# One tower on one core: the first stage's scores and projection become one 384-column product in f16 halves, and pooling reads projected rows

## What is computed

```python
A = jnp.tanh(jnp.einsum('bst,dt->bsd', text_embeddings, W_w) + W_b + b)
scores = jnp.einsum('bsd,od->bso', A, V_w)[..., 0] + V_b[0]
starts = jnp.arange(0, S - patch_len + 1, stride)      # patch_len 4, stride 2
idx = starts[:, None] + jnp.arange(patch_len)
sw = scores[:, idx]
w = jax.nn.softmax(sw, axis=-1)
xw = text_embeddings[:, idx]
attended = jnp.einsum('bpl,bplt->bpt', w, xw)
return jnp.einsum('bpt,dt->bpd', attended, P_w) + P_b
```

## Time and profile before

| | |
|---|---|
| median of 3 runs | 2064.79 us |
| the profiled execution | 2065.83 us, span 2063.9 us |
| setup | 0 to about 26 us of the span |
| first stage | 26.11 us (first load of x) to 459.98 us (last product ends) |
| TensorE busy over the span | 93% |
| VectorE, ScalarE, GpSimd busy | 72%, 68%, 56% |
| granted TensorE clock, mean | 0.973 of full speed |

### The profile page before, as it was taken

How to read it: one execution, slowest core, us unless ns; L and a number is a source line. 1 busy time by engine, 2 the same in 40 slices (tenths; PEclk the granted TensorE clock), 3 DMA queues, 4 the chain that set the end, 5 groups by cost and what they waited for, 6 DMA issues and landing times. The chain is left out here.

```text
span 2063.9 us, 60351 instructions
## 1 busy us (share of the span) xinstructions
PE 1911.3 (93%) x20800; PEld 1179.2 (57%) x20800; DVE 1478.8 (72%) x3636; ACT 1410.4 (68%) x2978; POOL 1162.1 (56%) x2198
## 2 busy tenths in 40 slices
PE   3999999993999999999999999999991899999998
PEld 3999999980444444444444444444441566666666
DVE  4555555553899999999999999999981455555554
ACT  1333333330889899899898998998982666666665
POOL 1111111127677777777777777777756565565561
PEclk9999999995999999999999999999996899999999
DMA  4444444421444444444444444444440332322322
GB/s 138 127 114 117 121 122 122 122 62 29 80 89 89 88 90 88 90 88 90 90 86 90 90 90 89 89 88 90 87 80 13 57 64 62 71 62 63 71 63 52
DMA packets 512122, 176.03 MB, mean 85 GB/s; under 512 B 452169, under 2 KB 511308, under 8 KB 512076
## 3 DMA queue, kind: packets, MB, share of 16 engines
q1 hardware_dynamic: 512075, 175.43, 38.7%
HBM read 53.79 MB, written 12.48 MB: 32 GB/s over the span
## 5 line engine op out<-in xcount | busy, mean ns | idle before, releaser
L692 DVE TENSOR_REDUCE tops<-p_maxa 128x6 f32<-128x762 f32 x512 | 483.0, 943 | 61.9 <-PE p_maxa L534 60.7
L605 PE MATMUL p_o<-probs,vn 127*32 127x256 f32 x6144 | 410.7, 385 | 0.2 <-DVE att L720 0.2
L530 PE MATMUL p_s<-qm,kt 32*128 32x256 f16 x3072 | 399.1, 275 | 1.3 <-ACT probs L649 0.4
L646 ACT ACTIVATE probs<-p_s 128x512 f32<-128x512 f32 x512 | 305.4, 596 | 108.4 <-PE p_s L530 95.6
L694 DVE TENSOR_REDUCE tops<-p_maxb 128x4 f32<-128x508 f32 x512 | 346.4, 676 | 0.0
L652 ACT ACTIVATE probs<-p_s 128x512 f32<-128x512 f32 x512 | 309.4, 604 | 0.0
L649 ACT ACTIVATE probs<-p_s 128x512 f32<-128x512 f32 x512 | 304.9, 596 | 0.3 <-PE p_s L530 0.2
L966 DVE TENSOR_TENSOR gel_lo<-gel,gel_hi 128x512 f16<-128x512 f32 x192 | 147.4, 768 | 215.7 <-ACT gel_hi L956 214.4
L534 PE MATMUL p_maxa<-kt,qt 24*128 24x256 f16 (+1 forms) x2048 | 284.1, 250 | 16.0 <-DMA kt<-qk 8.5
L360 POOL TENSOR_TENSOR diag<-ident,weight 128x256 f32<-128x256 f32 x128 | 78.9, 617 | 369.2 <-DVE band L339 328.3
L530 PEld LDWEIGHTS p_s<-qm,kt 32*128 32x128 f16 x3072 | 134.7, 91 | 182.9 <-issue 168.6
(11 more groups left out here) (186 smaller groups left out, 4522.3 us busy)
## 6 DMA issues: line engine op xcount, KB each, us to landing
xn<-in_xn SPq DMA_DIRECT2D x32, 768.0 KB, 6.3
xt_a<-in_xt SPq DMA_DIRECT2D x32, 512.0 KB, 4.4
out<-out_sb SPq DMA_DIRECT2D x32, 336.0 KB, 2.7
xt_b<-in_xt SPq DMA_DIRECT2D x32, 256.0 KB, 5.2
xt<-hx SPq DMA_TRANSPOSE x128, 2.3
kt<-qk SPq DMA_TRANSPOSE x128, 2.7
qt<-qk SPq DMA_TRANSPOSE x128, 2.4
qm<-qk SPq DMA_TRANSPOSE x128, 2.7
```

Of the source, the lines that this page charges most:

```text
L530: return nc.tensor.matmul(o, kt[full(j), r, kind, g, :], qm[full(j), r % 2, versions, g, :], start=True, stop=True, skip_group_check=True)
L605: last = nc.tensor.matmul(p_o[32 * j:32 * j + 32, blocks, :], vn[0:NP, r, src:src + 32], probs[0:NP, r % 2, QUAD * g + j, kind * 256:(kind ...
L646: nc.scalar.activation(probs[:, r % 2, h + 1, 0:512], p_s[1][:, :, :].rearrange("p x n -> p (x n)"), ACT.Exp, scale=SCALE).then_inc(act_e1 ...
L692: nc.vector.tensor_reduce(top[:, q, pair, 4:10], p_ma[:, 0:6, 0:NP], AX.X, ALU.max, negate=True).then_inc(dve_ma[u], 1)
```

## The change

W and P stand side by side as one matrix of 384 columns, so that one product gives a row's hidden values (columns 0 to 191) and its projected row (columns 192 to 383). The product runs in f16: x is split into a high and a low f16 half (x = hi + lo to about f32 accuracy), and so are the weights. Channels 0 to 127 take three products (hi x hi, hi x lo, lo x hi); channels 128 to 191 are loaded twice, on partitions 0 to 63 and 64 to 127, so that one stationary tile xb holds their low half above their high half and two products do; one more product of a tile of ones with bt adds the biases. So a half of a batch takes six products of 384 columns (L231 to L236 of the new kernel), and each of the two pa buffers is now two PSUM banks. ScalarE takes tanh of the first 192 columns of each half (L281) and copies the other 192 to zs (L283), a buffer of two groups. The pooling is then one product for each half, band times zs, straight into ph (L254); pt, att and the load of xn are gone.

The halves of x are made on the chip, one group ahead and two batches at a time, at k = 0 and at k = 2: ScalarE writes xa_hi (L270) and the masked high half of xt_b (L272, buffer tmp, named xb_hi in the program); GpSimd subtracts twice (L376, L379). The setup makes the f16 halves of the weights, and some counters are merged.

The core of the diff:

```diff
-                        pe.wait_ge(act_tanh, seen(n - 1))
+                        if k % 2 == 0:
+                            pe.wait_ge(pool_split, seen(i * 4 + 2 + 2 * (k // 2)))
+                        pe.wait_ge(act_z, seen(n - 1))
                         for odd in range(2):
-                            o = pa[two][:, odd * C:(odd + 1) * C]
-                            nc.tensor.matmul(o, xt_a[:, par, k, odd * 128:(odd + 1) * 128], t.wt_a[:, :], start=True, stop=False)
-                            last = nc.tensor.matmul(o, xt_b[:, par, k, odd * 128:(odd + 1) * 128], t.wt_b[:, :], start=False, stop=True)
+                            o, cols = pa[two][:, odd, 0:2 * C], slice(odd * 128, (odd + 1) * 128)
+                            nc.tensor.matmul(o, xa_hi[:, par, k, cols], ahi[:, :], start=True, stop=False)
+                            nc.tensor.matmul(o, xa_hi[:, par, k, cols], alo[:, :], start=False, stop=False)
+                            nc.tensor.matmul(o, xa_lo[:, par, k, cols], ahi[:, :], start=False, stop=False)
+                            nc.tensor.matmul(o, ones16[:, :], t.bt[:, :], start=False, stop=False)
+                            nc.tensor.matmul(o, xb[:, par, k, cols], bhi[:, :], start=False, stop=False)
+                            last = nc.tensor.matmul(o, xb[:, par, k, cols], blo[:, :], start=False, stop=True)
                         last.then_inc(pe_a, 1)
...
                         pe.wait_ge(dve_band, seen(u + 1))
-                        pe.wait_ge(act_att, seen(u - 1))
-                        for odd in range(2):
-                            nc.tensor.matmul(pt[two][:, 0:128], xn[:, par, k, odd * C:odd * C + CA], band[:, two, odd, :],
...
                         pe.wait_ge(act_h, seen(u - 1))
+                        for odd in range(2):
+                            last = nc.tensor.matmul(ph[two][:, 0:C], band[:, two, odd, :], zs[:, par, k, odd, :],
+                                                    start=(odd == 0), stop=(odd == 1))
+                        last.then_inc(pe_h, 1)
...
+            def split(i, par, half, part):
+
+                if within(i + 1, NG):
+                    two = slice(2 * part, 2 * part + 2)
+                    if part == 0:
+                        act.wait_ge(xt_in[1 - par], seen((half + par) * 48 + 48))
+                        act.wait_ge(pe_a, seen(i * G))
+                    nc.scalar.activation(xa_hi[:, 1 - par, two, :], xt_a[:, 1 - par, two, :], ACT.Copy)
+                    act.wait_ge(pool_split, seen(i * 4 + 4 + 2 * part))
+                    nc.scalar.activation(tmp[:, :, :], xt_b[:, 1 - par, two, :], ACT.Identity, scale=mask[:, 0:1], bias=none[:, 0:1])\
+                        .then_inc(act_split, 1)
...
+                        act.wait_ge(pe_h, seen(n - 2 * G + 1))
+                        nc.scalar.activation(zs[:, par, k, :, :], pa[two][:, :, C:2 * C], ACT.Copy).then_inc(act_z, 1)
+                    if k % 2 == 0:
+                        split(i, par, half, k // 2)
...
+                    if k % 2 == 0 and within(i + 1, NG):
+                        both = slice(k, k + 2)
+                        pool.wait_ge(act_split, seen(i * 2 + 3 + k // 2))
+                        nc.gpsimd.tensor_tensor(xa_lo[:, 1 - par, both, :], xt_a[:, 1 - par, both, :], xa_hi[:, 1 - par, both, :], ALU.subtract)\
+                            .then_inc(pool_split, 1)
+                        pool.wait_ge(pool_split, seen(i * 4 + 5 + k))
+                        nc.gpsimd.tensor_tensor(xb[:, 1 - par, both, :], xt_b[:, 1 - par, both, :], tmp[:, :, :], ALU.subtract)\
+                            .then_inc(pool_split, 1)
```

More of the change, by code:

```diff
@@ L109, in _ @@
         def _(dve):
+            nc.vector.memset(t.bt[:, :], 0.0)
             nc.vector.memset(t.bproj[:, :], 0.0).then_inc(cleared, 1)
@@ L118, in _ @@
             nc.vector.tensor_copy(t.b2[:, :], b2f[:, :])
+            for k in range(2):
+                nc.vector.tensor_copy(t.wt[k][:, :], wtf[k][:, :])
+                for row in (64 * k, 64 * k + 32):
+                    nc.vector.tensor_copy(t.bt[row:row + 1, :], btf[row:row + 1, :])
             nc.vector.tensor_copy(t.bproj[0:1, :], bprojf[0:1, :])
@@ L126, in _ @@
             nc.vector.tensor_tensor(t.w2_lo[:, :, :], w2f[:, :, :], t.w2_hi[:, :, :], ALU.subtract)
+            for k in range(2):
+                nc.vector.tensor_tensor(t.wt[2 + k][:, :], wtf[k][:, :], t.wt[k][:, :], ALU.subtract)
+                row = 64 * k + 32
+                nc.vector.tensor_tensor(t.bt[row:row + 1, :], btf[row:row + 1, :], t.bt[row:row + 1, :], ALU.subtract)
             nc.vector.tensor_tensor(t.b2[96:128, :], b2f[96:128, :], t.b2[96:128, :], ALU.subtract)
@@ L143, in tokenize @@
         xt_a = sb("xt_a", [CA, 2, G, S])
-        xt_b = sb("xt_b", [CB + 2, 2, G, S])
-        xn = sb("xn", [128, 2, G, 2 * C])
+        xt_b = sb("xt_b", [128, 2, G, S])
+        xa_hi, xa_lo, xb = (sb(n, [128, 2, G, S], F16) for n in ("xa_hi", "xa_lo", "xb"))
+        tmp = sb("xb_hi", [128, 2, S], F16)
+        mask, none = sb("mask", [128, 1]), sb("none", [128, 1])
+        ones16 = sb("ones_f16", [128, 128], F16)
+        zs = sb("zs", [128, 2, G, 2, C])
         tanhs = sb("tanhs", [128, 2, 2 * C])
@@ L156, in tokenize @@
         band = sb("band", [128, 2, 2, 128])
[L157 to L160, removed]
+        pa = [ps(f"pa{i}", [128, 2, 512]) for i in range(2)]
         ph = [ps(f"ph{i}", [128, 512]) for i in range(2)]
@@ L213, in _ @@
         def _(pe):
-            pe.wait_ge(ones, 3)
+            pe.wait_ge(ones, 4)
+            ahi, bhi, alo, blo = t.wt
             def body(i, par, half):
@@ L240, in body @@
                     if within(u, NB):
[L242 to L243 removed]
                         pe.wait_ge(dve_band, seen(u + 1))
[L245 removed]
+                        pe.wait_ge(act_h, seen(u - 1))
                         for odd in range(2):
[L247 to L260 removed]
+                            last = nc.tensor.matmul(ph[two][:, 0:C], band[:, two, odd, :], zs[:, par, k, odd, :],
+                                                    start=(odd == 0), stop=(odd == 1))
+                        last.then_inc(pe_h, 1)
             loop(pe, body)
@@ L274, in body @@
                         nc.scalar.activation(expo[:, :, :], shifted[:, :, :], ACT.Exp).then_inc(act_exp, 1)
-                    u = n - 2 * G
-                    if within(u, NB):
-                        act.wait_ge(pe_att, seen(u + 1))
-                        act.wait_ge(pe_h, seen(u - 1))
-                        nc.scalar.activation(att_a[:, two, :], pt[two][:, 0:128], ACT.Copy)
-                        nc.scalar.activation(att_b[0:CB, two, :], pt[two][0:CB, 128:256], ACT.Copy).then_inc(act_att, 1)
                     u = n - 2 * G - 1
@@ L288, in _ @@
         def _(dve):
-            nc.vector.memset(xt_b[CB:CB + 2, :, :, :], 1.0).then_inc(ones, 1)
-            nc.vector.memset(att_b[CB:CB + 1, :, :], 1.0).then_inc(ones, 1)
+            nc.vector.memset(ones16[:, :], 1.0).then_inc(ones, 1)
+            nc.vector.memset(none[:, :], 0.0)
+            nc.vector.memset(mask[0:CB, :], 0.0).then_inc(ones, 1)
+            nc.vector.memset(mask[CB:128, :], 1.0).then_inc(ones, 1)
             nc.vector.memset(expo[:, :, :], 0.0).then_inc(ones, 1)
@@ L1062, in audio_tower @@
             t.below, t.above = own("below", [128, 128]), own("above", [128, 128])
-            t.wt_a, t.wt_b = own("wt_a", [CA, C]), own("wt_b", [CB + 2, C])
-            t.pt_a, t.pt_b = own("pt_a", [CA, C]), own("pt_b", [CB + 1, C])
+            half = lambda name, shape: first.enter_context(nc.sbuf_tensor(name, shape, F16))
+            t.wt = [half("wt_" + n, [128, 2 * C]) for n in ("ahi", "bhi", "alo", "blo")]
+            t.bt = half("bt", [128, 2 * C])
             t.vw = own("vw", [128, C])
```

66 lines of the change are left out of this document (29 added, 37 removed).

## The result

The changed kernel takes 2099.76 us (median of 4 runs, 2096.75 to 2100.43) against 2064.88 us for the kernel before on the same chip: a ratio of 1.0161, with a 95% interval of 1.0143 to 1.0179. It is slower by 1.6%, and the forecast was 2099.

What follows compares the result with a forecast made beforehand. TensorE bounds the first stage before; afterwards a two-step chain through all four engines does. Thirty groups at 14.0 instead of 13.13 us give +26.1, the ends +8.6: +34.7, so 2099 us; forecast 2075 to 2120, full range 2058 to 2135.

Steps and rivals of the forecast that it cites:

- The ring: In the first stage, a two-step chain through TensorE, ScalarE, GpSimd and VectorE back to TensorE's pooling: 7.0 us, a group 14.0.
- uncollided sum: The chain's terms without engines holding each other up: 6.50 us for two steps, group 13.0; as a rival 2069 us, chance 0.13.
- the port: VectorE and GpSimd holding each other up when both read SBUF; forecast at 0.35 plus 0.15 us for two steps.
- from the band's end to zs: TensorE's pooling product of step 0, from the band until ScalarE's copy to zs can start: 1.07 us.
- the mask with its hand-over: ScalarE's masked half of x, 0.80 us, then GpSimd's wait for it, 0.07 us.
- the subtractions: GpSimd's two subtractions of 512 elements: 1.17 us each and 0.08 for a counter, 2.42 us together.
- The collisions: VectorE against GpSimd: 0.35 us for the second diag ahead of the band, 0.15 for a scoring instruction, added to 6.50.
- the rival built on the rule: VectorE–GpSimd meetings cost the whole instruction, 0.57 us for the second diag: group 15.0, 2129 us, chance 0.20.
- TensorE as the bound: Rival: first stage stays limited by TensorE, needing two steps below 5.4 us; group 10.8, 2003 us, chance 0.06.
- The rival of a slow clock: TensorE's waits drop its clock to 1.2 GHz: a step 5.2 us, group over 21, some 2350 us, chance 0.04.
- Busy share: Profile sign: TensorE about 75% busy between fill and drain of the first stage.
- The ends: Outside the 30 groups: setup +4, start +3.8, filling +5.8, draining -5 us; together +8.6.

Runs made afterwards that it cites:

- Experiments one and two: One: changed kernel with ScalarE's split ahead of its copy to zs, 2070.33 us. Two: changed kernel with both diags ahead of the subtractions, 2071.77 us.
- experiment four: The changed kernel with a third, unread GpSimd subtraction of 512 elements behind the first of each pair: 2167.91 us, ratio 1.0494 to the kernel before.
- experiment six: The changed kernel with V, the shift matrix and the softmax's small operands in PSUM, so no VectorE loop instruction reads two SBUF operands: 2071.65 us, ratio 1.0013.
- experiments five: The changed kernel with V, the scoring instruction's second operand, in a PSUM bank; the band keeps two SBUF operands: 2088.59 us, ratio 1.0095.
- experiment three: The changed kernel with ScalarE's split ahead of its copy to zs and both diags ahead of the subtractions: 2069.77 us, ratio 1.0020.
- Experiment eight: The changed kernel with split ahead of the zs copy, both diags ahead of the subtractions, and no two SBUF operands on VectorE: 2012.21 us, ratio 0.9727.
- experiment nine: The changed kernel with a one-column tanh ahead of ScalarE's first wait, to load the activation table earlier: 2097.98 us, one run.

## Why the prediction was right, and where it was not

**The ring: right in kind and in its uncollided sum.** The forecast held that TensorE's saving is lost because zs waits for the pooling product, and the split, diag and the band stand behind it. Experiments one and two cut the ring at two different places, and each gave back 28 to 29 us; experiment four lengthened it, and the time followed. The sum without collisions was 6.50 us, and where the port is out of the way (experiment six) a turn measures 6.48. Of its terms, from the band's end to zs (1.01 in the turn shown, 1.07 forecast), zs (0.38, 0.39), xa_hi (0.52, 0.53) and the mask with its hand-over (0.88, 0.87) are near; the subtractions took 1.155 and 1.159 us, where the difference of two rows of another shape gave 1.17.

**The collisions: right in cause, a little too dear.** The ring was put at 7.0 and is 6.84 to 6.92. The terms can be read from experiments five and six. Taking the scoring instruction out of the way shortened a turn by 0.11 us, where 0.15 stood; taking the band out as well shortened it by another 0.30 (half of 13.55 − 12.96), where 0.35 stood for the second diag ahead of it. The subtractions with their hand-overs to diag are 2.34 instead of 2.38 (2.42 less the overlap). Over 30 groups, 13.67 us each on average, it is +16.3 us where +26.1 stood: about 7 us because a group takes 13.77 instead of 14.0, and the other 3 because the forecast took the last of the 30 groups to be as long as the rest. It makes no more scores and took 11.85 us before and 10.82 after.

The way in which scoring enters was not the forecast's. It had the scoring instruction hold GpSimd up ahead of diag or of the second subtraction; the subtractions are not held up (1.155 and 1.159 us), but VectorE is, and in every second turn the band stands behind it in VectorE's own order. In the other turns VectorE is through before diag is. So the longest waits mostly hit instructions with slack behind them, and the price of the port was small for where it fell, not by its size. That was not in the forecast, and it is why experiment three missed: with the ring open, the same waits fall on the band.

The row of before showed one meeting. Of long subtractions the rule that the Trainium skill states (SBUF — State Buffer, Who interferes with whom) tells more than that row: who comes second waits nearly to the end of the first, as the scoring instruction does behind L379 (1.30 instead of 0.42), and the band pair behind both subtractions in experiment three (2.48 instead of 0.61). Beside the second diag the band pair loses only 0.25 to 0.34 us (0.86 and 0.95 instead of 0.61), where the rival built on the rule took 0.57, and its 15.0 us for a group did not come. (The words that the forecast quotes stand in the summary at the end of that page, the rule itself in the section named.) The same section says that a VectorE instruction with at most one SBUF input, outside the modes that use two ports, doesn't contend. Experiments five and six agree: 404 ns instead of 691, and 345 instead of 416, beside the same work of GpSimd.

**TensorE as the bound** was priced at a group of 10.8 us and 2003 us. Experiment eight has 10.97 and 2012.21, or 2008.5 by its ratio on the chip of the forecast; 30 groups at 0.17 us more make 5 us; the ends and the second stage enter as well, so this nearness too is in part a cancelling. The condition given for it, that the copy to zs be free of the pooling product, was not tried. Its nearest relative, the split free of it, is not enough: with experiment one alone the time is 2070.

**The clock.** The rival of a slow clock did not come: it was granted at 1.00 from 60 to 400 us. Experiment four shows that it was near, since 1.2 us more for a turn brought it to 0.92 there. The wait that the forecast gave it, 0.8 us in every second step, is not what its own sum says: a ring of 7.0 against 5.4 leaves 1.6. By the groups of 13.77 and 10.97 it is 1.4.

**Busy share.** 75% was forecast, 87% (294 of 340) is shown. A group takes 13.77 us, and experiment eight does the same products in 10.97, or 80%. Most of the rest is probably how the ends of matmuls are drawn, which no run isolates: a 384-column product shows as 0.33 us and the next starts 0.16 after it, so every stop of TensorE behind one counts some 0.16 us as busy. Here the share of busy time understates the idle time.

**The ends.** Setup (+4.8 for +4) and filling (+4.8 for +5.8) are near; the 0.5 us in the first for the larger loads had no row behind it. The start failed by 2.8 us: the sum left out the activation table's load, which had lain beside the first load of x in the kernel before and now stands behind the wait for it (1.28 us, experiment nine), and took the landing as unchanged, where it is 7.09 us after the issue and the product before the change began 5.65 after it. Draining gave back 6.9 for 5. Together +9.4 for +8.6.

**What came out by cancelling.** The 30 groups were put 9.8 us too high, and 8.9 us appeared behind the first stage, for which the forecast had nothing. That the median is within a microsecond of the forecast is owed to this. What is confirmed is the mechanism, with the ring to within 0.16 us of 7.0, not the last digit of the time.

## What to carry to other kernels

When work moves from a bound engine to idle ones, follow the chain through the order of each engine's instructions, and compare its length per turn with what the bound engine then needs: here 6.5 us against 5.5 measured, with every engine but TensorE below 75% busy. Two limits of the same height hide one another: cutting the ring gave some 28 us, freeing the port 31, both together 82 to 90, and either experiment alone would have suggested that little is left. Where GpSimd gets long instructions, put one operand of what VectorE does beside them into PSUM, and put instructions that wait for nobody ahead of the one that waits.

## What the runs showed of the hardware

A VectorE instruction with one operand in PSUM was no slower than with both in SBUF: scoring 404 to 412 ns (417 alone before), the band 344 to 345 (348). A load of the activation table stands where the first activation of the program needs it, so a wait ahead of that activation puts 1.28 us on the path. A stage that no edit touches differed by 4 to 7 us between two programs, and by up to 2 us between two executions of one; the cause of the first is open. TensorE's granted clock stayed at 1.00 with about 1.4 us lost in each turn of 6.9 us (changed kernel), and fell to 0.50 for some 3.4 us, once in 17 to 24, with turns of 8.1 us (experiment four).
